# Spreading the attention map in four transfers of 256 KB in place of two of 512 KB

## The reference, cut to what matters

```python
for t in range(STEPS):                       # STEPS = 3
    attn = softmax(einsum('nd,bsnd->bns', q, k) / 4, axis=-1)      # 2 heads, over the 1024 pixels
    pooled = einsum('bns,bsnd->bnd', attn, v)
    weights = softmax(where(allowed, pooled @ Wmlp, -1e9) / 1.5)   # 4 experts, the best two are kept
    wsel = top2(weights)
    x_mod = x * (1.0 + attn.mean(heads) * S * softplus(alpha))     # one factor for each pixel
    y = sum(wsel[:, e] * conv3x3(x_mod, We[e]) for e in range(4))
    x = y
```

## Time and profile before

| | |
|---|---|
| median of 3 runs | 3884.75 us |
| the profiled execution | 3886.65 us, its span 3884.5 us |
| first stage | about the first 640 us of the span |
| busy over the span | PE 93%, DVE 95%, ACT 78%, POOL 84% |
| `map_all<-map_scratch` | 48 transfers of 512 KB, median 5.8 us from issue to landing |
| granted TensorE clock | 0.994 of full speed over the span |

### The profile page before, as it was taken

How to read it: one execution, slowest core, us unless ns; L and a number is a source line. 1 busy time by engine, 2 the same in 40 slices (tenths; PEclk the granted TensorE clock), 3 DMA queues, 4 the chain that set the end, 5 groups by cost and what they waited for, 6 DMA issues and landing times. The chain is left out here.

```text
span 3884.5 us, 36761 instructions
## 1 busy us (share of the span) xinstructions
PE 3609.6 (93%) x9740; PEld 1388.3 (36%) x9740; DVE 3698.2 (95%) x3395; ACT 3031.5 (78%) x4614; POOL 3264.2 (84%) x1542
## 2 busy tenths in 40 slices
PE   6999998999999999999999999999999999999998
PEld 2232222333333333333333333333333333333333
DVE  6878777999999999999999999999999999999998
ACT  5677776788888888888888888888888888888885
POOL 2222223999999999999999999999999999999998
PEclk8999999999999999999999999999999999999999
DMA  4242335999889899989999989989999998999986
GB/s 115 55 123 55 111 112 177 363 349 346 344 345 355 345 348 347 350 348 346 347 354 351 351 349 348 347 347 345 356 351 350 348 349 346 345 348 354 353 339 251
DMA packets 203137, 1181.22 MB, mean 304 GB/s; under 512 B 30929, under 2 KB 31729, under 8 KB 68785
## 3 DMA queue, kind: packets, MB, share of 16 engines
q1 hardware_dynamic: 200128, 1177.64, 80.3%
q10 hardware_dynamic: 2800, 1.23, 0.1%
HBM read 1144.03 MB, written 34.73 MB: 303 GB/s over the span
## 5 line engine op out<-in xcount | busy, mean ns | idle before, releaser
L1565 POOL TENSOR_TENSOR read<-state,bc_all 128x1024 f32<-128x1024 f32 x1024 | 2395.8, 2363 | 108.1 <-DVE state L1629 105.2
L1629 DVE TENSOR_TENSOR_SCAN state<-decays,p_drive 128x1024 f32<-128x1024 f32 x1024 | 2289.0, 2273 | 18.6 <-ACT p_drive L1464 4.8
L1334 PE MATMUL p_y<-read,ident 128*128 128x512 f32 x4096 | 1955.7, 604 | 16.0 <-POOL read L1565 8.8
L1456 ACT ACTIVATE decays<-dt,wa 128x496 f32<-128x496 f32 x2048 | 1336.9, 702 | 75.2 <-DVE state L1629 72.7
L1334 PEld LDWEIGHTS p_y<-read,ident 128*128 128x128 f32 x4096 | 739.5, 190 | 1053.4 <-issue 774.2
L1616 DVE TENSOR_TENSOR p_drive<-bc_all,p_dtx 128x1024 f32<-128x1024 f32 x768 | 908.6, 1213 | 0.0
L1582 POOL TENSOR_TENSOR pool_drive<-dtx,bc_all 128x1024 f32<-128x1024 f32 x256 | 603.7, 2358 | 3.7 <-DMA bc_all<-bc_scratch 3.7
L1464 ACT COPY p_drive<-pool_drive 128x1024 f32<-128x1024 f32 x256 | 260.8, 1019 | 415.0 <-DVE state L1629 415.0
L785 POOL TENSOR_TENSOR pad<-map_all,xc 128x512 f32<-128x512 f32 x96 | 130.5, 1391 | 484.1 <-DMA map_all<-map_scratch 484.1
L566 PE MATMUL p_conv<-pad,wm 128*64 128x512 f32 x1152 | 268.7, 601 | 23.9 <-issue 23.8
L1330 PE MATMUL p_y<-xconv,d_diag 128*128 128x512 f32 x256 | 143.9, 644 | 156.6 <-DVE gated L1639 156.6
(11 more groups left out here) (163 smaller groups left out, 3067.9 us busy)
## 6 DMA issues: line engine op xcount, KB each, us to landing
bc_all<-bc_scratch SPq DMA_DIRECT2D x1024, 1024.0 KB, 6.9
map_all<-map_scratch SPq DMA_DIRECT2D x48, 512.0 KB, 5.8
norm_rows<-xn SPq DMA_DIRECT2D x32, 280.0 KB, 6.1
norm_in<-norm_rows SPq DMA_DIRECT2D x64, 140.0 KB, 7.8
norm_in<-norm_rows SPq DMA_DIRECT2D x64, 139.8 KB, 7.9
fresh<-in_x SPq DMA_DIRECT2D x32, 256.0 KB, 6.7
x<-in_x SPq DMA_DIRECT2D x32, 256.0 KB, 3.4
mid_x<-x SPq DMA_DIRECT2D x32, 256.0 KB, 6.6
```

Of the source, the lines that this page charges most:

```text
L1334: nc.tensor.matmul(p_y[:], ident[:], read[:, s % DEEP, :], start=False, stop=(s == N - 1)).then_inc(y_added, 1)
L1456: nc.scalar.activation(decays[:, s % DEEP, :].rearrange("p (q t) -> p q t", t=SIDE)[:, :, 1:], dt[b][:, :, 1:], ACT.Exp, scale=wa[m][:, s: ...
L1565: nc.gpsimd.tensor_tensor(read[:, s % DEEP:s % DEEP + 2, :], state[:, s % DEEP:s % DEEP + 2, :], bc_all[s // CHUNK][:, :, 1, :], ALU.mult) ...
L1629: nc.vector.tensor_tensor_scan(state[:, at:at + 2, :].rearrange("p s n -> p (s n)"), decays[:, at:at + 2, :].rearrange("p s n -> p (s n)") ...
```

## The change

Each half's transfer is cut in two: first both halves of the map for images 0 and 1, then both for images 2 and 3, in 4 KB to each of 64 partitions. Each pair has its own semaphore. POOL waits for the first pair before image 0 and for the second before image 2.

```diff
-    map_loaded = sem("s1_map_loaded")
+    map_loaded = [sem(f"s1_map_loaded{n}") for n in two]
...
-            for h in two:
-                rows = map_scratch[TEAM * h:TEAM * h + TEAM].rearrange("a n -> (a n)")
-                sp.dma_start(map_all[CH * h:CH * h + CH, :, :].rearrange("p a n -> p (a n)"),
-                             rows.partition_broadcast(CH)).then_inc(map_loaded, 16)
+            for n in two:
+                for h in two:
+                    at = TEAM * h + 2 * n
+                    rows = map_scratch[at:at + 2].rearrange("a n -> (a n)")
+                    sp.dma_start(map_all[CH * h:CH * h + CH, 2 * n:2 * n + 2, :].rearrange("p a n -> p (a n)"),
+                                 rows.partition_broadcast(CH)).then_inc(map_loaded[n], 16)
...
-            pool.wait_ge(map_loaded, 32 * P + 32)
             for a in team:
+                if a % 2 == 0:
+                    pool.wait_ge(map_loaded[a // 2], 32 * P + 32)
```

## The result

The changed kernel takes 3896.15 us (median of 8, 3894.16 to 3900.07), the kernel before beside it 3885.51 (median of 8): 1.0028 times as long, 95% interval 1.0018 to 1.0038, so 10.6 us slower; 3894 was predicted. The first profiled execution took 3900.07 us (span 3897.7), the longest of the eight. Lines have moved: L566, L578, L699, L724, L785, L862 of before are L568, L580, L701, L726, L788, L865.

What follows compares the result with a forecast made beforehand. Two chains end at `conv_anti`: map, POOL, PE, and mix, ACT, shift. 13.7 - 4.9 - 14.4 - 2.7 = -8.3, put at 9 us slower: median 3894 us, range 3880 to 3903.

Steps and rivals of the forecast that it cites:

- The first pair's landing: Map transfers: the new 512 KB pair lands when the first transfer did before, 2.24 us before POOL's old start.
- The middle value: Of three landing times in round 2, the one set by bytes: 91.22, between 90.64 and 93.46.
- The estimate of 6.4 us: Issue to landing for two transfers one after the other, each paying about 2 us fixed, at about 218 GB/s.
- Plain rounds: Rounds 1 to 4, 9, 10, 15, 16, 21, 22: PE's wait for `pad` goes in full, 13.7 us won.
- Rounds with k = 1 or 2: Six rounds of later bodies: two multiplications get in before the last L862, `conv_anti` starts later; 4.9 us lost.
- The caution that an arrival a little sooner meets one mix more: Round 20 and others of its kind: arriving 0.2 us sooner meets one mix more, at 1.0; total put at 9.
- Rounds with k = 5 or 0: Rounds 5, 6, 11, 12, 17, 18: all four multiplications precede the last L862, delaying ACT and copies; 14.4 us lost.
- Round 23: POOL arrives at 615.46 as the first L855 ends; three multiplications get in, 3.1 us; 2.7 us lost.
- Round 0: PE's 2.0 us wait, its longest; POOL's arrival among six mixes gives 1 lost to 2 won, taken as 0.
- Harmless POOL: Rival, chance 0.08: POOL comes early without meeting mixes, PE's 23.8 us of waits go; 3861 us.
- Halves as long as wholes: Rival, chance 0.08: half-size transfers take as long, the pair lands at 93.46 as before; 3885 us, no change.
- a pair that lands later: Rival, chance 0.12: landing 0.7 to 1.3 us later than the first transfer before, fewer mixes met; 3881 us.

Runs made afterwards that it cites:

- e8: Changed kernel with ACT's step output and image 0's shift copies put ahead of the scaling for image 3; 3885.32 us, ratio 0.9999.
- e6b: Changed kernel with six mix operations of images 0 and 1 (rounds 0 to 22) reading a PSUM column, not the SBUF running sum; 3853.60 us.
- second profile: A further profiled execution of the changed kernel, unaltered; this execution took 3896.13 us.
- e2: Changed kernel with POOL waiting before image 1 until the second of the two last mix operations is done; 3868.70 us, ratio 0.9956.
- e10: Changed kernel unaltered, timed and profiled again; 3896.32 us, ratio 1.0029 to the kernel before.

## Why the prediction was right, and where not

- *The first pair's landing.* The middle value was right: POOL starts 5.04 us after the first issue in round 2, and on the mean of rounds 0 to 22 it starts 2.26 us sooner in the first profile and 2.24 in the second (2.24 predicted). Two transfers of 256 KB, issued one behind the other, land about when one of 512 KB did. The estimate of 6.4 us worked out from the Trainium skill (SBUF — State Buffer, "The DMA setup-cost knee") for two transfers one after the other is too long. The measurement decides, and it fits two transfers that overlap and don't pay the fixed part twice.
- *Plain rounds.* 14.1 and 14.5 won, for 13.7. The step as told was too uniform: pairs of L865 took 2.7 us in rounds 3, 4, 9, 10, 16 and 22 of the first profile and 1.67 in 1, 2, 15 and 21. It made no difference, as ACT had the slack.
- *Rounds with k = 1 or 2.* Two pushes of 1.03 and a wait of 1.42 for the copies, as worked out; 4.4 and 5.7 for 4.9. The caution that an arrival a little sooner meets one mix more came true: in round 13 the first profile has two mixes pushed and 0.77 lost, the second three and 1.86. There POOL starts 0.77 us after the first L858, just before the second:

```profile
369.93 2.72 DVE L858 SCALAR_TENSOR_TENSOR mix<-we_sb,wsel,mix 128x640 f32<-128x640 f32 x2
...
370.70 6.74 POOL L788 TENSOR_TENSOR pad<-map_all,xc 128x512 f32<-128x512 f32 x4 [21.71 <-DMA map_all<-map_scratch]
...
372.58 3.71 DVE L865 SCALAR_TENSOR_TENSOR wm<-we_sb,wsel,mix 128x640 f32<-128x640 f32 x2
```

- *Rounds with k = 5 or 0.* 2.0 to 2.3 in rounds 5, 11, 12 and 17, and 2.9 to 3.3 in 6 and 18, for 2.06 and 3.1. The size was right; of the reason half was missing. The prediction named the way over the mix, ACT and the copies alone. In the first profile PE first stands 2.06 us before `conv_main` for the mixed weights themselves, and then, in round 5, waits 1.39 for the copies as it did before the change; and DVE's own queue carries the delay to the next round as well (e8).
- *Round 23.* 1.7 for 2.7. POOL started 1.03 us after the first L858, where 0.81 was reckoned (615.46 - 614.65), so that two got in, not three: 2 x 1.03, less the 0.35 that ACT no longer waits for `pad`.
- *Round 0.* Between its bounds (+0.9, +0.7), and less than that is the change's, as most of it is there before the round's map (above). From the first small matmul on, the round loses 0.05 us in the first profile and 0.4 in the second: the earlier landing wins nothing here, because POOL does not get in. Here the turn-taking goes the other way. The first multiplication of round 0 in the changed kernel, with DVE's last two mixes beside it, and the multiplications of the same round in e6b:

```profile
40.17 5.64 POOL L788 TENSOR_TENSOR pad<-map_all,xc 128x512 f32<-128x512 f32 x1 [30.89 <-DMA map_all<-map_scratch]
...
43.01 1.66 DVE L865 SCALAR_TENSOR_TENSOR wm<-we_sb,wsel,mix 128x640 f32<-128x640 f32 x2
```

```profile
39.79 4.98 POOL L788 TENSOR_TENSOR pad<-map_all,xc 128x512 f32<-128x512 f32 x4 [30.51 <-DMA map_all<-map_scratch]
```

  POOL waits for all six mixes and is done 1.1 us after them (45.81 against 44.67); the mixes lose nothing. In the kernel before it was the same: POOL's first multiplication of round 0 took 3.51 us from 41.08 on, and the mixes ended at 43.46. With one SBUF input on DVE the same start takes 1.25 us an image. Why DVE keeps its turn in round 0 and gives it up in the others stays open.
- *The rivals.* Harmless POOL: 3861 was reckoned without meetings, and 3853.6 came when they were taken away (e6b, which takes those of the kernel before away too). Halves as long as wholes, and a pair that lands later: the landing excludes both.
- *The sum.* That 8.3 were reckoned and the second profile has 8.1 up to the table load is in part luck: the rounds with k = 1 or 2 lose 0.8 more than forecast and round 0 0.7, the plain rounds win 0.8 more and round 23 loses 1.0 less.
- *Left over.* The medians differ by 10.6 to 10.9. Beside the 8.1 us, the second profile's span grows by 1.1 behind the table load (3893.7 against 3884.5, 9.2 in all) and its time outside the span by 0.3; and the profiled execution of the kernel before (3886.65) lies 1.1 above its median. What the 1.1 us behind the table load are was not followed up; in the first profile the same stretch is 0.6 shorter.

## What to carry to other kernels

A buffer that is ready sooner lets an engine start sooner, and what it then meets is a part of the price: look which instructions run on the other engine in the window into which the start moves, and whether one excludes the other. Where it does, early work is worth having only for the piece that somebody waits for; let the first piece in and hold the rest with a wait that is already met by the time it counts (e2: one wait more turned 10.6 us lost into 18 won). And when an order is altered to free one queue, look at the next two queues: here the gain of ACT's new order ended at DVE's queue and at ACT's own.

## What was not expected of the hardware

- GpSimd and VectorE, each with two SBUF inputs, take turns at instruction boundaries: each multiplication of 1.25 us that gets in costs VectorE 1.03. With one of VectorE's inputs in PSUM, mixes and multiplications ran together at 0.8 and 1.25 us each (e6b). In round 0 VectorE didn't yield at all and GpSimd's operation took 5.64 us.
- After a wait of PE of the same length (1.42 us) the granted clock fell in one execution of the same kernel (3.51 us for eight matmuls) and stayed full in another (1.94). Within one execution (e10) it fell after a wait of 2.06 us in round 12 and not after one of 3.14 in round 11 (4.14 and 2.80 us for twelve matmuls).
